# A graph network with a routed expert layer: TensorE's two products of an expert block, one block apart

## The reference

```python
logits = xt @ Wr + br                                  # 8 experts
top_p, top_idx = top_k(softmax(logits), 2)             # each token goes to 2 of them
weights = top_p / top_p.sum(axis=-1, keepdims=True)
xe = xn * ln_g[e] + ln_b[e]                            # xn: the normalized token
h = gelu(xe @ W1[e] + b1[e])                           # 256 -> 1024
y = h @ W2[e] + b2[e]                                  # 1024 -> 256
out = (weights[:, :, None] * y_of_the_two).sum(axis=1)
```

## Time and profile before

| what | us |
|---|---|
| device time, median of 3 runs | 3797.17 |
| lowest and highest run | 3793.64 and 3798.28 |
| span of the profiled execution, first to last instruction | 4365.6 |
| PE busy in it | 3253.1 (75%) |
| POOL busy in it | 2531.6 (58%) |
| mean granted TensorE clock in it | 0.861 |
| first to last instruction of the expert blocks in it | 1372.06 to 2286.45 |

### The profile page before, as it was taken

One profiled execution on the slowest core, in us unless ns is written; L12 is line 12 of the kernel. 1 busy time (PEld: TensorE's weight loads), 2 busy tenths in 40 slices (PEclk: granted clock), 3 DMA queues, 4 the chain that ended last, 5 costly groups with the idle time before them and its releaser, 6 DMA issues. The chain is left out here.

```text
span 4365.6 us, 47498 instructions
## 1 busy us (share of the span) xinstructions
PE 3253.1 (75%) x15077; PEld 2484.5 (57%) x15077; DVE 1790.8 (41%) x5335; ACT 1496.2 (34%) x2892; POOL 2531.6 (58%) x2604
## 2 busy tenths in 40 slices
PE   1455565555446989988886798987989868999868
PEld 1344444444335777776764576655666645666547
DVE  4355565534353111111117333343333435676664
ACT  3233333323323112121115244443444434555520
POOL 6666666666643656565546666665666656666620
PEclk6677777777767999999988899988999979999978
DMA  6343334334312545554437454554544534555452
GB/s 194 111 122 109 117 115 118 116 108 120 101 40 98 176 157 179 172 185 156 157 124 269 124 146 136 149 159 116 144 138 142 166 107 143 150 153 152 135 175 103
DMA packets 396972, 609.34 MB, mean 140 GB/s; under 512 B 81648, under 2 KB 295319, under 8 KB 395943
## 3 DMA queue, kind: packets, MB, share of 16 engines
q0 software_dynamic: 115808, 279.40, 22.6%
q1 hardware_dynamic: 274182, 317.02, 22.4%
q10 hardware_dynamic: 6720, 9.74, 0.7%
HBM read 509.58 MB, written 96.33 MB: 139 GB/s over the span
## 5 line engine op out<-in xcount | busy, mean ns | idle before, releaser
L2983 POOL DMA_INDIRECT rows_h<-table,step_src x1138 | 1105.8, 972 | 688.6 <-issue 342.5
L3025 PE MATMUL bank_g<-rows_hl,counts_h 128*128 128x512 f32 x3773 | 1049.8, 422 | 89.0 <-issue 45.4
L975 POOL DMA_INDIRECT rows_r<-table,step_src x782 | 749.6, 959 | 405.2 <-issue 214.1
L3025 PEld LDWEIGHTS bank_g<-rows_hl,counts_h 128*128 128x128 f32 x3773 | 721.3, 194 | 301.9 <-issue 101.0
L1000 PE MATMUL bank_r<-rows_r,hots_r 128*128 128x257 f32 x1564 | 473.4, 457 | 457.4 <-ACT rows_r L985 227.3
L1000 PEld LDWEIGHTS bank_r<-rows_r,hots_r 128*128 128x128 f32 x1564 | 340.1, 227 | 567.6 <-ACT rows_r L985 261.6
L3184 ACT ACTIVATE counts_h<-piece_h 128x896 fp32r<-128x896 uint8 x539 | 498.1, 945 | 458.8 <-PE bank_g L3025 223.3
L1901 POOL DMA_INDIRECT kept_A<-one_d,place_d x424 | 420.7, 992 | 127.4 <-issue 127.1
L2016 PE MATMUL pY_e<-w_e,h_e 128*128 128x256 f32 x1680 | 421.7, 410 | 76.7 <-ACT h_e L1982 54.4
L1011 DVE TENSOR_SCALAR hots_r<-lane,step_dst 128x128 f32<-128x128 f32 x782 | 210.3, 289 | 593.3 <-remote 365.2
L1982 ACT ACTIVATE h_e<-pH_e,prm_e 128x256 f32<-128x256 f32 (+1 forms) x456 | 179.6, 455 | 733.7 <-PE pH_e L2005 486.5
(11 more groups left out here) (397 smaller groups left out, 3864.9 us busy)
## 6 DMA issues: line engine op xcount, KB each, us to landing
w_e<-in_L_ffn_W SPq DMA_DIRECT2D x114, 1024.0 KB
piece_h<-kept_A SPq DMA_DIRECT2D x539, 112.0 KB
kept_A<-zero_r SPq DMA_DIRECT2D x189, 112.0 KB
rows_h<-table,step_src POOLq DMA_INDIRECT x1138
table<-ACC SPq DMA_DIRECT2D x51, 256.0 KB
kept_sw<-vec_g SPq DMA_DIRECT2D x49, 256.0 KB
rows_r<-table,step_src POOLq DMA_INDIRECT x782
b_e<-in_L_ffn_b SPq DMA_DIRECT2D x57, 128.0 KB
```

The source lines that it names most:

```text
L975: nc.gpsimd.indirect_dma_start(out=r["rows"][:, x, 0:D], out_offset=None, in_=r["table"][:, :], in_offset=bass.IndirectOffsetOnAxis(ap=c[" ...
L2983: nc.gpsimd.indirect_dma_start(out=d["rows"][:, x, :], out_offset=None, in_=tables[l - 1][:, :], in_offset=bass.IndirectOffsetOnAxis(ap=c[ ...
L3025: mm = pe.matmul(sums, d["counts"][:, n % CV, x % PC, :], both.both(t), start=(x == 0 and i >= RINGED[l]), stop=(x == NT - 1))
```

## The change

The first product of block b+1 now stands ahead of the second product of block b, so PE's program is: first product of b+1, turn of b+2, second product of b. For this `h` gets two places by b % 2 (ACT waits for the second product of b-2 before it writes), the first product waits for the gelu of the block before it (its banks `pH` are read there), and the turn waits for `xe` of the block before it. W1 and W2 are loaded apart: W1 of block b once the first product of b-3 is done, W2 of block b-1 once `y` of b-4 is there. POOL gathers one block further ahead, and its iteration b is now the tokens of b+3, the results of b, then the edges of b. Two semaphores of `invert` are used on by `experts`, with their counts as a base (`since`).

```diff
-def load_expert(sp, ins, moe, m, b, s_y=None):
...
+def load_first(sp, ins, moe, m, b):
+    q, e = b % WEIGHTS, expert_at(sp, moe, b)
...
+    sp.dma_start(m["w1"][:, q, :, :], w1_d[:, bass.ds(e, 1), :, :].rearrange("p o k h -> p (o k) h")).then_inc(m["s_w1"][q], 16)
+def load_second(sp, ins, moe, m, b):
...
+    sp.dma_start(m["w2"][:, q, :, :], w2_d[:, bass.ds(e, 1), :, :].rearrange("p o j d -> p (o j) d")).then_inc(m["s_w2"][q], 16)
+    sp.dma_start(m["b2"][:, q, :], ins["L0_ffn_b2"][bass.ds(e, 1), :].to_broadcast([P, D])).then_inc(m["s_w2"][q], 16)
 def experts(nc, ins, dram, c, moe, d, m, sb, pb, sem):
         @block.sync
             for b in range(WEIGHTS, NBLK):
-                sp.wait_ge(s_mm2, b - WEIGHTS + 1)
-                load_expert(sp, ins, moe, m, b, s_y)
+                sp.wait_ge(s_mm1, (b - WEIGHTS + 1) * (HJ // 2))
+                load_first(sp, ins, moe, m, b)
+                if b > WEIGHTS:
+                    sp.wait_ge(s_y, halves_before(b - WEIGHTS))
+                    load_second(sp, ins, moe, m, b - 1)
+            sp.wait_ge(s_y, halves_before(NBLK - WEIGHTS))
+            load_second(sp, ins, moe, m, NBLK - 1)
         @block.vector
             inputs(0)
+            inputs(1)
             for b in range(NBLK):
-                if b + 1 < NBLK:
-                    inputs(b + 1)
+                if b + 2 < NBLK:
+                    inputs(b + 2)
         @block.scalar
+                if b > 1:
+                    act.wait_ge(s_mm2, since + b - 1)
                 for j in range(HJ // 2):
                     act.wait_ge(s_mm1, b * (HJ // 2) + j + 1)
-                        a = act.activation(h[:, k, 0:w], pH[j][:, n * BR:n * BR + w], ACT.Gelu,
+                        a = act.activation(h[:, b % 2, k, 0:w], pH[j][:, n * BR:n * BR + w], ACT.Gelu,
         @block.tensor
             def turn(b):
                 pe.wait_ge(s_tok[q], 16 * (halves_before(b, 2) + n))
+                if b > 0:
+                    pe.wait_ge(s_xe, 2 * b)
...
+            def first(b):
+                pe.wait_ge(s_xe, 2 * b + 2)
+                pe.wait_ge(s_w1[q], 16 * (b // W + 1))
                 for j in range(HJ // 2):
+                    if b > 0:
+                        pe.wait_ge(s_h, (b - 1) * (HJ // 2) + j + 1)
...
+            def second(b):
+                pe.wait_ge(s_w2[q], 32 * (b // W + 1))
                 if b > 0:
                     pe.wait_ge(s_y, halves_before(b))
+                pe.wait_ge(s_h, (b + 1) * (HJ // 2))
...
+            turn(0)
+            first(0)
+            turn(1)
+            for b in range(NBLK):
+                if b + 1 < NBLK:
+                    first(b + 1)
+                if b + 2 < NBLK:
+                    turn(b + 2)
+                second(b)
         @block.gpsimd
-            for b in range(4):
+            for b in range(3):
                 tokens(b)
-                if b > 1:
-                    results(b - 2)
             first = halves_before(2)
-            for b in range(2, NBLK):
-                if b + 1 < NBLK:
+            for b in range(NBLK):
+                if b + 3 < NBLK:
+                    tokens(b + 3)
+                results(b)
+                if 2 <= b < NBLK - 1:
                     for n in range(*(late * (halves_before(x) - first) // (COLS - 1 - first) for x in (b, b + 1))):
                         edges(nc, g, dram, d, EARLY[2] + n)
-                if b + 2 < NBLK:
-                    tokens(b + 2)
-                results(b)
```

More of the change, by code:

```diff
@@ L1801, in invert @@
         away = sb("away_i", [P, 3, P], F32, ctx)
-        s_c, s_v, s_hot, s_mm, s_act = sem("i_const"), sem("i_v"), sem("i_hot"), sem("i_mm"), sem("i_act")
+        s_c, s_v, s_hot, s_mm, s_act = sem("i_const"), sem("i_v"), m["s_hot"], m["s_mm"], sem("i_act")
         AWAY = [n for n in range(2 * NT) if squared(n)]
@@ L1809, in _ @@
             for b in range(WEIGHTS):
-                load_expert(sp, ins, moe, m, b)
+                load_first(sp, ins, moe, m, b)
+                load_second(sp, ins, moe, m, b)
         @block.gpsimd
@@ L1924, in experts @@
     with ExitStack() as ctx:
-        w1, w2, b2, s_w = m["w1"], m["w2"], m["b2"], m["s_w"]
+        w1, w2, b2, s_w1, s_w2 = m["w1"], m["w2"], m["b2"], m["s_w1"], m["s_w2"]
         tok = sb("tok_e", [P, 2, 2, D], F32, ctx)
@@ L1928, in experts @@
         xe = sb("xe_e", [P, 2, KD, BR], F32, ctx)
-        h = sb("h_e", [P, HJ, BR], F32, ctx)
+        h = sb("h_e", [P, 2, HJ, BR], F32, ctx)
         y = sb("y_e", [P, 2, 2, D], F32, ctx)
@@ L1935, in experts @@
         s_st = [sem(f"e_store{q}") for q in range(2)]
-        s_prm, s_T, s_xe, s_mm1, s_h, s_mm2, s_y = (sem("e_prm"), sem("e_T"), sem("e_xe"), sem("e_mm1"), sem("e_h"),
-                                                    sem("e_mm2"), sem("e_y"))
+        s_xe, s_mm1, s_h, s_y = sem("e_xe"), sem("e_mm1"), sem("e_h"), sem("e_y")
+        s_T, s_mm2, since = m["s_hot"], m["s_mm"], 2 * NT
         block = ctx.enter_context(nc.Block())
@@ L1955, in inputs @@
                     v.wait_ge(s_h, b * 4 - 4)
-                v.tensor_copy(prm[:, q, :], moe["prm"][:, bass.ds(e, 1), :].rearrange("p o n -> p (o n)")).then_inc(s_prm, 1)
-                v.wait_ge(s_prm, b + 1)
-                v.wait_ge(s_T, b + 1)
+                v.tensor_copy(prm[:, q, :], moe["prm"][:, bass.ds(e, 1), :].rearrange("p o n -> p (o n)")).then_inc(s_xe, 1)
+                v.wait_ge(s_xe, 2 * b + 1)
+                v.wait_ge(s_T, since + b + 1)
                 for k in range(KD):
@@ L1964, in _ @@
             inputs(0)
+            inputs(1)
             for b in range(NBLK):
-                if b + 1 < NBLK:
-                    inputs(b + 1)
+                if b + 2 < NBLK:
+                    inputs(b + 2)
                 if b > 1:
                     v.wait_ge(s_st[b % 2], 16 * halves_before(b, 2))
-                v.wait_ge(s_mm2, b + 1)
+                v.wait_ge(s_mm2, since + b + 1)
                 for m in range(block_of(b)[2]):
@@ L1994, in turn @@
                 mm.then_inc(s_T, 1)
-            turn(0)
-            for b in range(NBLK):
+            def first(b):
                 q, halves = b % W, block_of(b)[2]
-                pe.wait_ge(s_xe, b + 1)
-                pe.wait_ge(s_w[q], 48 * (b // W + 1))
+                pe.wait_ge(s_xe, 2 * b + 2)
+                pe.wait_ge(s_w1[q], 16 * (b // W + 1))
                 for j in range(HJ // 2):
+                    if b > 0:
+                        pe.wait_ge(s_h, (b - 1) * (HJ // 2) + j + 1)
                     for n in range(2):
@@ L2007, in _ @@
                     mm.then_inc(s_mm1, 1)
-                if b + 1 < NBLK:
-                    turn(b + 1)
+            def second(b):
+                q, halves = b % W, block_of(b)[2]
+                pe.wait_ge(s_w2[q], 32 * (b // W + 1))
                 if b > 0:
                     pe.wait_ge(s_y, halves_before(b))
+                pe.wait_ge(s_h, (b + 1) * (HJ // 2))
                 for j in range(HJ):
-                    if j % 2 == 0:
-                        pe.wait_ge(s_h, b * (HJ // 2) + j // 2 + 1)
                     for m in range(halves):
-                        mm = pe.matmul(pY[m][:, 0:D], h[:, j, m * P:(m + 1) * P], w2[:, q, j, :],
+                        mm = pe.matmul(pY[m][:, 0:D], h[:, b % 2, j, m * P:(m + 1) * P], w2[:, q, j, :],
                                        start=(j == 0), stop=(j == HJ - 1))
                 mm.then_inc(s_mm2, 1)
+            turn(0)
[7 more added lines that the diff above has]
+                second(b)
         @block.gpsimd
@@ L2024, in tokens @@
                 if b > 1:
-                    g.wait_ge(s_T, b - 1)
+                    g.wait_ge(s_T, since + b - 1)
                 for m in range(n):
@@ L2161, in mixture @@
         m = dict(w1=sb("w1_e", [P, WEIGHTS, KD, HID], F32, ctx), w2=sb("w2_e", [P, WEIGHTS, HJ, D], F32, ctx),
-                 b2=sb("b2_e", [P, WEIGHTS, D], F32, ctx), s_w=[sem(f"e_w{q}") for q in range(WEIGHTS)])
+                 b2=sb("b2_e", [P, WEIGHTS, D], F32, ctx), s_w1=[sem(f"e_w1{q}") for q in range(WEIGHTS)], s_w2=[sem(f"e_w2{q}") for q in range(WEIGHTS)], s_hot=sem("i_hot"), s_mm=sem("i_mm"))
         invert(nc, ins, dram, c, moe, d, m, sb, pb, sem)
@@ L2167, with expert_at @@
 WEIGHTS = 3
-def load_expert(sp, ins, moe, m, b, s_y=None):
-    q, i = b % WEIGHTS, block_of(b)[0]
-    e = sp.value_load(moe["expert"][0:1, i:i + 1], min_val=0, max_val=NE - 1)
+def expert_at(sp, moe, b):
+    i = block_of(b)[0]
+    return sp.value_load(moe["expert"][0:1, i:i + 1], min_val=0, max_val=NE - 1)
+def load_first(sp, ins, moe, m, b):
+    q, e = b % WEIGHTS, expert_at(sp, moe, b)
     w1_d = ins["L0_ffn_W1"].rearrange("e (k p) h -> p e k h", p=P)
+    sp.dma_start(m["w1"][:, q, :, :], w1_d[:, bass.ds(e, 1), :, :].rearrange("p o k h -> p (o k) h")).then_inc(m["s_w1"][q], 16)
+def load_second(sp, ins, moe, m, b):
+    q, e = b % WEIGHTS, expert_at(sp, moe, b)
```

(2 more changed lines are left out.)

1 line of the change is left out of this document (removed).

## The result

The changed kernel takes 3813.89 us (median of 4 runs, 3811.76 to 3817.99), the kernel before 3796.12 us (4 runs, 3793.64 to 3798.28): a ratio of 1.0052, with a 95% interval of 1.0038 to 1.0066. It is 17.8 us slower (the interval allows 14 to 25), where I had forecast 9.6 over 3797.2.

What follows compares the result with a forecast made beforehand. It took PE to bound the timed expert blocks without gaps, near 751 us. Terms 1.2 + 1.2 + 7.2 = +9.6 us over 3797.2 gave 3807 us, likeliest 3802 to 3812, over all 3775 to 3818.

Steps and rivals of the forecast that it cites:

- late words: In expert blocks, PE's word reaches other engines 6 to 12 us late; taken as added by watching, absent from timed runs.
- Steady state: Undisturbed expert blocks: same PE work and no idle time to fill, added waits already met: 0 us.
- Start: Behind the turn of block 1, PE waits for xe of block 1 with no second product over it: +1.2 us.
- End on PE: Second products of 55 and 56 stand together, and the latter waits for y of 55: +1.2 us.
- End on POOL: Seven edges stand between the results of 55 and 56, delaying the last results: +7.2 us.
- Tokens: Token waits around half blocks: three tight places instead of two, against less crowded loads; +16 to -14, taken as 0 us.
- the likeliest case: The forecast itself for the whole kernel: +5 to +14 us, 3802 to 3812 us, chance 0.50.
- the wide range: Range over all cases for the whole kernel: 3775 (about 0.12 below) to 3818 us (about 0.07 above).
- The waits are real: First rival: timed expert blocks have the late words too, so 30 us before second products go: 3777 us; chance 0.23.
- Slower still: Rival: POOL falls behind at each half block, +8 to +16 us beside the 9.6: 3815 to 3823 us; chance 0.12.
- No change: Rival: half-block token waits go with the split loads, 8 us, net +1.6: 3799 us; chance 0.15.
- What would show it: Signs: last results about 8 us after PE's end, 1.2 us gap at start, profiled stage near 900 us.

Runs made afterwards that it cites:

- experiment 4: The kernel before with POOL's tokens of b+2 put ahead of its edges: 3777.58 us, ratio 0.9960.
- experiment 6: The changed kernel with the seven edges of block 55 issued behind the results of block 1: 3804.97 us, ratio 1.0030.
- experiment 1: The kernel before, unchanged, profiled anew (the second profile of before): 3794.53 us, one run.
- experiment 5: The changed kernel with POOL's order of before (edges of b, tokens of b+3, results of b): 3794.74 us; then with tokens, edges, results: 3782.40 us.

## Why the prediction was right, and where a term was off

*What bounds the kernel.* PE nearly without gaps, a timed stage near 751 us: the second profile of before has the blocks at 770.7 us. Beside the 751 stand the token waits (12.9), the start, and the slower products named under experiment 4. Right in what it concluded; wrong in its reason. I wrote that the late words are "something that watching adds". Watching alone doesn't add them: the second profile is a watched execution of the same kernel, its span is its device time less 2.0 us, and no second product waits in it. They belonged to one execution, whose device time isn't known, and what disturbed it stays open. Of the two places of the Trainium skill that I weighed against the trace, "Runtime: NRT & Kernel Launch", section "The ~15µs preamble/postamble breakdown", has a profile's total some 6 us above the execution time. Here the span lies 2.0 us below the device time of its own execution (3792.5 against 3794.53); but a span from the first to the last instruction is not that total, so no run here tests the figure. "NOTIFIC — the notification-queue block", section 10, has an implicit trace record cost the engine no cycles; no kernel was timed with and without records, and the second profile, with 0.0 us of idle PE before second products, doesn't speak against it. What told the trace from the timed runs was the 568 us between them.

*Steady state, 0 us.* Right: PE stood idle 0.0 us before second products in before, and 1.0 in after, all of it at the end.

*Start, +1.2.* Measured 2.3 - 1.2 = 1.1. *End on PE, +1.2.* Measured 0.96.

*End on POOL, +7.2.* Measured 7.96 - 0.81 = 7.15, and experiment 6 shows it as a term of its own: without it the loss falls from 17.8 to 9.1 us (8.7, give or take some 7 by the two intervals).

*Tokens, 0 us.* This is the step that failed. I had said that two tight places would become three, found no row that leaned either way, and took the middle of +16 and -14. It measured 30.5 - 21.8 = +8.7 us, and experiment 1 shows one wait behind a half block where I had two. In after there is a second one at each of eight half blocks, 1.0 to 1.7 us each and 10.7 in all, while the first ones fell from 12.9 to 10.8. The order of POOL's program did lean. In after the six edges of block 13 stand ahead of the tokens of block 17; in experiment 5, where PE's order is the same, the three of the half block 14 stand there, and the second wait is gone. Three edges are 3.8 us, more than any of these waits. I had counted POOL's calls around a half block, but had not followed which edges stand ahead of which tokens in the new order. The gain that I set against it, split loads that crowd less, shows as no more than 1.1 us: experiment 5, with the split loads and before's POOL order, has 11.8 us of token waits behind half blocks, where before has 12.9.

The four sum to 1.1 + 1.0 + 7.2 + 8.7 = 18.0 us, against 17.8 measured; an agreement this close is luck, with an interval of 14 to 25 us and profiles that differ by a few us from one execution to the next. With experiments 5 and 6, 16 of the 18 us are POOL's order: edges that stand ahead of something PE or the barrier waits for. The other 2 are PE's own start and end.

So the direction was right, and so were three of the four terms. The total was not: the likeliest case gave +5 to +14, or 3802 to 3812 us, and the time is 3813.89, which only the wide range to 3818 holds.

*The rivals.* "The waits are real" fell with experiment 1. "Slower still", to which I gave 0.12, is what happened: POOL behind at half blocks, 8.7 us for a price of 8 to 16, and 17.8 in all for its 17.6 to 25.6. "No change" fell: 10.8 of the 12.9 us of before's token waits stayed, and the second ones came on top.

*What would show it.* The tail (8 us) and the start were as said. That the profiled stage would stay near 900 us with idle PE before first products was wrong, by the same error as above: it took 781.1.

## What to carry to other kernels

Set the span of a profile against the timed runs before reading a wait out of it: here the widest idle time of PE in these blocks, 76.7 us, was 0.0 in the next profile of the same kernel. Where one in-order queue carries both work that someone waits for and work that no one waits for, put the first ahead: moving two lines on POOL was worth 16 us, a reordering of PE nothing that could be measured. And count such a queue block by block around irregular blocks, and at the end, where nothing is left to hide under.

## What the runs showed of the hardware

Indirect DMAs that POOL issues back to back keep one cadence, 0.94 to 1.01 us and 0.30 before the next, in the disturbed execution (0.970 on average over 316 edges) as in the others, and whether they gather or scatter rows of 256 elements or scatter single ones. A gather of 128 rows lands 2.7 to 6.7 us after its issue in after, where 1 MB loads run, and 2.7 to 4.4 us with these loads cut to 64 KB.
